# The last stage's heads: spread through DRAM by DMA, or by selection products on TensorE

## What is computed

```python
h = x @ Wm + bm                         # 256 -> 256
t = h.reshape(bs * L_ * H, HD)          # H = 8 heads of HD = 32
w = softmax(t @ expert_emb)             # 16 experts
topw, topi = top_k(w, 2)
hmid = gelu(einsum('td,edi->tei', t, W1) + b1)     # 32 -> 128, each expert
eo = einsum('tei,eio->teo', hmid, W2) + b2         # 128 -> 32
comb = sum of eo[topi] * topw
out = comb.reshape(bs, L_, d) @ Wo + bo
x = layernorm(x + out)
```

## Time and profile before

| | us |
|---|---|
| median of 3 runs | 3492.32 |
| the profiled execution | 3488.05 |
| its span, first to last instruction | 3486.0 |
| last stage, from its first DMA (2691.39) to the end | 794.6 |

### The profile page before, as it was taken

One profiled execution on the slowest core, in us unless ns is written; L12 is line 12 of the kernel. 1 busy time (PEld: TensorE's weight loads), 2 busy tenths in 40 slices (PEclk: granted clock), 3 DMA queues, 4 the chain that ended last, 5 costly groups with the idle time before them and its releaser, 6 DMA issues. The chain is left out here.

```text
span 3486.0 us, 39510 instructions
## 1 busy us (share of the span) xinstructions
PE 3114.9 (89%) x11504; PEld 1685.3 (48%) x11504; DVE 2607.9 (75%) x3783; ACT 2287.1 (66%) x3239; POOL 2357.0 (68%) x1680
## 2 busy tenths in 40 slices
PE   3589999999999999998789999989976799999998
PEld 1156666666666666776334433443422333333332
DVE  5988888788888787554699999999996444444443
ACT  2466666766666666664666667567653488888887
POOL 3578788888888877775477888787784144444443
PEclk7689999999999999999899999999998799999999
DMA  2034444444444444553122222222221122222222
GB/s 94 13 101 127 114 127 124 121 124 117 121 124 122 123 116 123 145 147 109 49 70 70 72 68 67 73 70 69 68 73 58 48 99 99 105 105 105 103 102 86
DMA packets 199618, 335.38 MB, mean 96 GB/s; under 512 B 21379, under 2 KB 57380, under 8 KB 199020
## 3 DMA queue, kind: packets, MB, share of 16 engines
q1 hardware_dynamic: 199404, 332.86, 31.3%
HBM read 325.69 MB, written 7.09 MB: 95 GB/s over the span
## 5 line engine op out<-in xcount | busy, mean ns | idle before, releaser
L1439 POOL TENSOR_TENSOR c_hc<-c_h,c_c_rep 128x1024 f32<-128x1024 f32 x256 | 603.4, 2361 | 207.8 <-DVE c_h L1490 150.3
L1920 POOL TENSOR_TENSOR d_acc<-d_acc,d_prod 128x512 f32<-128x512 f32 x240 | 319.1, 1329 | 472.5 <-DVE d_prod L1988 471.7
L1490 DVE TENSOR_TENSOR_SCAN c_h<-c_decay,c_carry,c_v_ps 128x512 f32<-128x512 f32 x512 | 627.9, 1261 | 0.0
L1880 ACT ACTIVATE d_hmid<-d_up,d_b 128x1024 f32<-128x1024 f32 x512 | 540.2, 1113 | 77.1 <-PE d_up L1781 76.7
L1340 ACT ACTIVATE c_decay<-c_dt,c_a_cols 128x512 f32<-128x512 f32 x512 | 356.6, 718 | 337.0 <-DVE c_h L1490 319.9
L1190 PE MATMUL c_y_ps<-c_hc,ident 128*128 128x512 f32 x1024 | 507.1, 619 | 68.4 <-POOL c_hc L1439 56.4
L704 POOL TENSOR_TENSOR ab_inner_low<-ab_inner,ab_inner_high 128x512 fp32r<-128x512 f32 x264 | 342.3, 1297 | 234.3 <-ACT ab_inner_high L570 232.9
L559 ACT ACTIVATE ab_gate_ps<-ab_gate_ps,ab_raw_d 128x512 f32<-128x512 f32 x264 | 174.5, 661 | 464.7 <-PE ab_gate_ps L411 463.4
L1988 DVE SCALAR_TENSOR_TENSOR d_prod<-d_eo,d_b,d_w_rep 128x512 f32<-128x512 f32 x240 | 180.2, 751 | 314.9 <-PE d_eo L1791 182.2
L782 DVE SCALAR_TENSOR_TENSOR ab_tanh<-ab_tanh,ab_gate_ps 128x512 f32<-128x512 f32 x264 | 180.6, 684 | 313.0 <-ACT ab_tanh L564 312.1
L686 POOL TENSOR_TENSOR ab_hc<-ab_h,ab_c_rep 128x512 f32<-128x512 f32 x256 | 330.9, 1293 | 104.3 <-DVE ab_h L767 98.8
(11 more groups left out here) (239 smaller groups left out, 6611.7 us busy)
## 6 DMA issues: line engine op xcount, KB each, us to landing
ab_raw_gu<-in_b_experts SPq DMA_DIRECT2D x264, 256.0 KB, 3.4
ab_w_rep<-ab_w_scratch SPq DMA_DIRECT2D x264, 256.0 KB, 3.6
c_c_rep<-c_c_scratch SPq DMA_DIRECT2D x256, 256.0 KB, 3.1
d_w_rep<-d_w_scratch SPq DMA_DIRECT2D x256, 256.0 KB
ab_raw_d<-in_b_experts SPq DMA_DIRECT2D x264, 129.0 KB, 2.1
ab_raw_x<-in_xT SPq DMA_DIRECT2D x32, 256.0 KB, 4.8
out<-xT SPq DMA_DIRECT2D x8, 512.0 KB, 3.4
xT<-in_xT SPq DMA_DIRECT2D x1, 3072.0 KB, 13.1
```

Source lines behind the costliest of these rows:

```text
L1439: nc.gpsimd.tensor_tensor(hc[:, q % HC], h[:, q % HR], c_rep[:, q % BC].unsqueeze(1).broadcast_to([P, PAIR, CH]), ALU.mult).then_inc(hc_re ...
L1490: nc.vector.tensor_tensor_scan(out=h[:, q % HR, m, :], data0=decay[:, i % DEC, :], data1=v_ps[m][:], initial=carry[:, i:i + 1], op0=ALU.mu ...
L1880: nc.scalar.activation(hmid[:, (2 * q + r) % HM], up_ps[r][:], ACT.Gelu, bias=b1[:, e:e + 1]).then_inc(gelu_ready, 1)
L1920: nc.gpsimd.tensor_tensor(acc[:, s, g, :], acc[:, s, g, :], prod[:, q % PR, :], ALU.add).then_inc(add_ready, 1)
```

## The change

The selection products (L1754), their matrices and the copies (L1937) go. Instead SP stores the whole tile `parts` of chunk c+1 to DRAM (one DMA, 128 partitions, 8 KB each, 1 MB), waits until it has landed, and loads `heads` from there by eight DMAs of 256 KB: for each of four blocks of 32 partitions and each group of 4 heads, 32 rows of 4 times 2 KB. The store stands on SP's queue behind `spread` of step 9, the loads behind `spread` of step 12. The logits (step 13) wait for all eight loads. ScalarE's first write to `parts` waits until the store of the chunk before has landed. In the stage's start the load of `sel` (512 KB) and its cast go too.

```diff
+            def store_parts(c, s):
+                sp.wait_ge(low_ready, (c + 1) * GROUPS)
+                sp.dma_start(parts_dram[s], parts[:].bitcast(F32)).then_inc(parts_stored, 16)
+
+            def load_heads(c, s):
+
+                sp.wait_ge(parts_stored, (c + 1) * 16)
+                for block in range(NQ):
+                    rows = parts_dram[s, :, :, block // 2, :].rearrange("(j p) g t -> p g j t", j=HPG)
+                    for g in range(GROUPS):
+                        sp.dma_start(heads[block * DH:(block + 1) * DH, s, g * HPG:(g + 1) * HPG, :].bitcast(F32),
+                                     rows[:, g]).then_inc(head_ready, 16)
+
...
                 for q in range(NU):
                     spread(c, s, q)
+                    if q == Q_KEEP_PARTS and not last:
+                        store_parts(c + 1, 1 - s)
+                    if q == Q_HEADS and not last:
+                        load_heads(c + 1, 1 - s)
...
-                elif i < LOGITS:
-                    g, j = (i - HEAD0) // HPG, (i - HEAD0) % HPG
-                    for part in range(2):
-                        last = nc.tensor.matmul(work_ps[:], sel[:, j, part, :], parts[:, g, part, :],
-                                                start=(part == 0), stop=(part == 1))
                 elif i == LOGITS:
+                    pe.wait_ge(head_ready, (c + 1) * NQ * GROUPS * 16)
...
+                if g == 0 and not is_int(c, 0):
+                    act.wait_ge(parts_stored, c * 16)
...
-            def keep_head(c, s, i):
-
-                dve.wait_ge(work_ready, c * ITEMS + HEAD0 + i + 1)
-                nc.vector.tensor_copy(heads[:, s, i, :], work_ps[:]).then_inc(head_ready, 1)
```

More of the change, by code:

```diff
@@ L1610, in layer1_experts @@
     HM, UP, EO, PR, WR = 4, 2, 2, 4, 8
-    HEAD0, LOGITS, TURN, BACK = GROUPS, GROUPS + HEADS, GROUPS + HEADS + 1, GROUPS + HEADS + 2
+    LOGITS, TURN, BACK = GROUPS, GROUPS + 1, GROUPS + 2
     ITEMS = BACK + 1
     Q_OUT, Q_MEAN, Q_CENTRE, Q_SQUARE, Q_VAR, Q_SCALE = 18, 20, 21, 23, 24, 20
-    Q_HALF, Q_HIGH, Q_LOW, Q_HEAD, Q_COPY = 0, 0, 1, 4, 5
+    Q_HALF, Q_HIGH, Q_LOW, Q_KEEP_PARTS, Q_HEADS = 0, 0, 1, 9, 12
     Q_LOGITS, Q_KEEP_LOGITS, Q_TURN, Q_MAX, Q_EXP, Q_PICK, Q_BACK, Q_KEEP_WEIGHTS = 13, 13, 15, 16, 17, 18, 26, 26
@@ L1632, in layer1_experts @@
         norm_ps = ctx.enter_context(nc.psum_tensor("d_norm", [P, CH], F32))
+        parts_dram = nc.dram_tensor("d_parts_scratch", (2, P, GROUPS, 2, CH), F32, kind="Internal").ap()
         w_dram = nc.dram_tensor("d_w_scratch", (2, GROUPS, HPG, E, CH), F32, kind="Internal").ap()
@@ L1642, in layer1_experts @@
         heads_b = sb("heads_b", [P, GROUPS])
-        sel_raw = sb("sel_raw", [P, HPG, 2, P])
-        sel = sb("sel", [P, HPG, 2, P], F32R)
         parts = sb("parts", [P, GROUPS, 2, CH], F32R)
@@ L1662, in layer1_experts @@
         loaded = sem("loaded")
-        sel_ready = sem("sel_ready")
+        parts_stored = sem("parts_stored")
         split_ready = sem("split_ready")
@@ L1693, in _ @@
             sp.dma_start(heads_b[:], w["heads_b"]).then_inc(heads_loaded, 16)
-            sp.dma_start(sel_raw[:], w["sel"]).then_inc(heads_loaded, 16)
             sp.dma_start(raw[:], w["w1"].rearrange("p e i -> p (e i)")).then_inc(loaded, 16)
@@ L1726, in store_out @@
                 sp.dma_start(k["out"][:, :, bass.ts(c, CH)], xT[:, :, bass.ts(c, CH)]).then_inc(k["stored"], 16)
+            store_parts(0, 0)
+            load_heads(0, 0)
             store_weights(0, 0)
@@ L1740, in product @@
                     pe.wait_ge(wt_ready, c)
-                elif i <= HEAD0:
+                elif i <= LOGITS:
                     pe.wait_ge(high_ready, c * GROUPS + i)
                     pe.wait_ge(low_ready, c * GROUPS + i)
-                elif i <= LOGITS:
-                    pe.wait_ge(head_ready, c * HEADS + i - HEAD0)
-                if i < HEAD0:
+                if i < LOGITS:
                     for half in range(2):
@@ L1777, in up @@
                 if q == 0 and r == 0:
-                    pe.wait_ge(head_ready, (c + 1) * HEADS)
+                    pe.wait_ge(head_ready, (c + 1) * NQ * GROUPS * 16)
                 pe.wait_ge(gelu_ready, c * 2 * NU + 2 * q + r + 1)
@@ L1827, in chunk @@
                             product(c + 1, 1 - s, (q - Q_HALF) // 2)
-                        if Q_HEAD <= q < Q_HEAD + HEADS:
-                            product(c + 1, 1 - s, HEAD0 + q - Q_HEAD)
                         if q == Q_LOGITS:
@@ L1837, in _ @@
             pe.sem_inc(down_ready, HM // 2)
-            pe.wait_ge(heads_loaded, 3 * 16)
+            pe.wait_ge(heads_loaded, 2 * 16)
             for i in range(ITEMS):
-                if i == HEAD0:
-                    pe.wait_ge(sel_ready, 1)
                 if i == LOGITS:
@@ L1897, in chunk @@
                             keep_weights(c + 1)
-            act.wait_ge(heads_loaded, 3 * 16)
+            act.wait_ge(heads_loaded, 2 * 16)
             act.sem_inc(gelu_ready, UP)
@@ L2000, in chunk @@
                             low(c + 1, (q - Q_LOW) // 2)
-                        if Q_COPY <= q < Q_COPY + HEADS:
-                            keep_head(c + 1, 1 - s, q - Q_COPY)
                     if q >= 1:
@@ L2042, in split_weights @@
                             nc.vector.tensor_copy(emb[rows, g, g * E:(g + 1) * E], emb_raw[rows]).then_inc(emb_ready, 1)
-            dve.wait_ge(heads_loaded, 3 * 16)
-            nc.vector.tensor_copy(sel[:], sel_raw[:]).then_inc(sel_ready, 1)
+            dve.wait_ge(heads_loaded, 2 * 16)
             dve.sem_inc(prod_ready, EO)
@@ L2052, in _ @@
             low(0, 1)
[L2053 to L2056, removed]
+            for i in range(3):
+                split_weights(2 + i)
             dve.wait_ge(emb_ready, 3 * HEADS)
@@ L2134 @@
         sel_sum[:, kk, :] = (row[:, None] // N_STATE + DPT * kk) == np.arange(QUAD)[None, :]
-    sel_parts = np.zeros((P, NQ, 2, P), np.float32)
-    for j in range(NQ):
-        for part in range(2):
-            sel_parts[:, j, part, :] = ((row[:, None] // QUAD == j) & (row[None, :] // (2 * QUAD) == part)
-                                        & (row[:, None] % QUAD == row[None, :] % QUAD))
     w_bc = np.stack([np.tile(x["L0_attn_W_B"].T, (1, DPT)), np.tile(x["L0_attn_W_C"].T, (1, DPT)),
@@ L2175 @@
         "d_b2": np.tile(x["L1_ffn_b2"].T, (4, 1)),
-        "d_heads_w": x["L1_ffn_Wm"], "d_heads_b": cols(x["L1_ffn_bm"]), "d_sel": sel_parts,
+        "d_heads_w": x["L1_ffn_Wm"], "d_heads_b": cols(x["L1_ffn_bm"]),
         "d_out_w": x["L1_ffn_Wo"], "d_out_b": cols(x["L1_ffn_bo"]),
```

## The result

The changed kernel takes 3612.53 us (median of 5 runs, 3612.28 to 3613.1), the kernel before 3492.32. The ratio is 1.0344, with a 95% interval of 1.0331 to 1.0357: 120 us slower. The forecast was 77 us slower, at 3569 us, with a range from 3532 to 3602 us, so the measured time lies outside it. The direction was right, and so was the reason, a full DMA queue. The size was not: a chunk costs 6.6 us more than the sum said, because the transfers of the heads also slow the w_rep loads, which the sum left out.

A forecast was written before the change was run, and what follows sets the result against it. The four DMA engines carrying w_rep become the bound: 2747.4 - 4 + 7 x (88.4 + 12.1) + 115.5 = 3562.4, +76 us against the span of 3486.0; added to the median 3492.3, 3569 us. Range 3532 to 3602 us.

The forecast's parts named there:

- The second limit: Four DMA engines carrying all w_rep loads: a queue cycle of 88.4 us a chunk, 2.6 us behind the 91.0 of compute.
- Rival (b): New transfers fit beside the w_rep loads, so compute is the bound: 3472 us, chance 0.07.
- Removed products: TensorE, steps 4 to 11: without selection products 2.3 us less a chunk, compute cycle 88.8 us, lost because the queue bounds.
- The store, 2.7 us: Store of parts, 1 MB on 128 partitions: adds 2.7 us a chunk on the four narrow engines.
- The heads' own part, 9.4 us: Eight loads of heads, 2.10 MB at 224 GB/s as for 64 partitions: 9.4 us a chunk on the narrow engines.
- The step that failed: Time added to the narrow DMA queue by store and loads: 12.1 us a chunk, making its cycle 100.5 us.
- rival (d): Heads' loads disturb the w_rep loads as well: 16 us a chunk, 3596 us, chance 0.15.
- A sign read wrongly: Steps 4 to 11: waits there for w_rep would show that the queue was not the bound.
- The slump after the heads: w_rep loads after the heads' loads: possibly half rate once more for some 3.5 us, costing 1.7 us.
- The start: Before chunk 0: without sel and with the new store and loads, a gain of 4 us.
- The wait at the logits: TensorE at L1758, before step 13's down: waits for the heads about 12 us in each of seven chunks.
- TensorE's clock: TensorE after its stop at the logits: may run slower, compute cycle a few us over 88.8, hidden by the 12 us.

The follow-up runs named there:

- e7: Changed kernel with routing weights stored four times, so that w_rep loads run on sixteen engines instead of four: 3472.47 us, ratio 0.9945 to the kernel before.
- e6: Kernel before with routing weights stored four times, so that w_rep loads run on sixteen engines: 3492.26 us, ratio 1.0006.
- e1: Changed kernel without the loads of heads for chunks 1 to 7, the store of parts kept: 90.67 us a chunk, 3508.39 us.
- e4: Changed kernel with the eight loads in another order, blocks 0, 2, 1, 3 for each group of heads: 102.53 us a chunk, 3582.08 us.
- e2: Changed kernel without the stores of parts for chunks 1 to 7, loads of heads kept: 104.35 us a chunk, 3591.47 us.
- e9: Changed kernel without later stores, the heads' loads reading 4 repeated rows so only the four narrow engines carry them: 108.20 us a chunk, 3632.25 us.
- e5: Changed kernel without later stores, the eight loads going onto all 128 partitions instead of 32: 96.79 us a chunk, 3545.22 us.

## Why the prediction was right in kind and wrong in size

- **The second limit.** Right. That four engines carry w_rep, at 100 GB/s, and are full for nearly the whole chunk decided the case. e7 is the proof: only the loads of w_rep, and the four stores that they need, are changed, and the sign turns. Rival (b), that the transfers fit in, is out, and the page's DMA share of 2 tenths was no slack.
- **Removed products.** Two steps without a product now take 4.61 us (below, chunk 4), as forecast, and this gain is lost at the logits.

```profile
3205.75 1.06 PE L1802 MATMUL d_eo<-d_hmid,d_w 128*32 128x512 f32 x8
...
3210.36 1.06 PE L1802 MATMUL d_eo<-d_hmid,d_w 128*32 128x512 f32 x8
```

  What it is worth where it can show is e7 against e6: 91.0 - 88.5 = 2.5 us a chunk, for which the sum had 2.3.
- **The store, 2.7 us.** Measured 2.3 (e1).
- **The heads' own part, 9.4 us.** Measured 9.7 in the windows of chunk 4. The rows of a load of 64 partitions were the right neighbours for it. They were so in part by luck: in e4's order of the same loads the same part runs at 74 to 98 GB/s, so the rate is not that of the form alone. By the prediction's estimate from the Trainium skill, "SBUF — State Buffer", section "Door 1: The DMA port swizzle", it was 9.6 us; the trace agrees with 9.7.
- **The step that failed** is the size of the added queue time: "the four narrow ones are busy 2.7 + 9.4 = 12.1 us longer a chunk". Its two terms measured 2.3 and 9.7, 12.0 together, but the whole is 18.7 us. It left out that the twelve free engines, which it counted as costing nothing, slow w_rep while they run ahead with their three quarters of the heads: some 6.3 us a chunk (e2 and e9). The prediction had this as rival (d), "14 to 16", with 0.15, and priced it too low there too. A chunk is 107.05 - 100.5 = 6.6 us longer than forecast, 7 x 6.6 = 46 us; by the medians 43 us are missing, and the end of the stage, 3.5 us shorter than the sum had it, accounts for most of the difference. That sixteen engines, the heads beside w_rep, fall to some 160 GB/s stood in no row of before. Why they do so stays open; e4 and e5 show that it depends on the partitions and on the order.
- **A sign read wrongly.** The prediction said that waits for w_rep in steps 4 to 11 would mean that the queue is not the bound. In chunk 4 weigh of step 11 waits 6.13 us for it, and the queue is the bound all the same: this wait is the missing term.
- **The slump after the heads** didn't come: from 3235 on the windows stand at 100 GB/s.
- **The start.** 3.1 us gained, 4 forecast.
- **The wait at the logits.** Forecast as 12 us in each of seven chunks; the list of waits has 120.4 us in seven for TensorE, 17 each. Right place, and longer by the same missing term.
- **TensorE's clock.** The prediction's "may run slower for a while" is seen: the granted clock is 0.50 from 3221 to 3241 in chunk 4, after TensorE has stood since 3218. It was said to be hidden, and the trace agrees. From 3235 to 3279 the DMA share is 0.26 or more in every window of 1 us, and the store of the weights, issued at 3279.65, lets the next chunk's first load go only at 3284.85: 5.2 us, where it takes 2.0 alone. So the queue still had work in line. No run tests the clock by itself.

## What to carry to other kernels

A mean DMA share of 0.26 may be four engines that are full. Compare the share of a steady stretch with k/16, the share of k full engines, and look at how long a small DMA on the same queue takes from issue to landing: here 12.2 us instead of 2.0 said that it stood in line. Before moving work from an engine to DMA, add the transfer's part on the fullest DMA engine, at the rate of the nearest shape, to that engine's cycle, and price what the free engines do to the full ones while they run beside them. If a transfer repeats a few rows over many partitions, the rows can be stored more often, so that its outermost dimension becomes 16: with this the same change gained 20 us instead of losing 120. By itself it gained nothing (e6), since there compute was the bound.

## What was not expected of the hardware

- Transfers of sixteen engines onto 32 partitions slow w_rep loads of four engines to a half or less: 6.9 and 5.1 us for 256 KB instead of 2.6. All sixteen together moved 147 to 201 GB/s at full share in chunk 4. The same loads alone, ahead of chunk 0, moved 195 to 229 from 2720 to 2728, as here:

```profile
2725.00:2726.00 1.00, 0.50 1.06 199
```

- 2.10 MB by four engines alone, in packets of 8 KB, cost 19.8 us a chunk, by sixteen in packets of 2 KB 16.0 us. Four times as many engines gave a fifth less.
- The order in which blocks of 32 partitions are loaded was worth 4.5 us a chunk, with no byte more or less.
